# Audio tower on one core: first norm's statistics ahead of the second state scan, transposed rows evicted ahead of the output's exponentials, last tile's sums three chunks earlier

## The chip, the cores and the metric

One core of a Trainium2 chip runs the whole kernel as one program on TensorE (PE), VectorE (DVE), ScalarE (ACT), GpSimd (POOL) and SyncE (SP), which only issues DMAs. The metric is device microseconds (us); the median over several executions is compared. The profile is one more execution, taken with the hardware profiler.

## The reference, cut to what matters

The input is 32 sequences of 750 frames with 256 channels. Two wavelet levels (8 taps, stride 2) give 192 tokens a sequence, 6144 in all. Then come a layer norm, a gated linear recurrence over time, and a second layer norm with a mixture of 8 experts of which each token takes 2.

```
h = tok(x)                                   # two strided convolutions over time
h = h + attn(layernorm(h))
h = h + ffn(layernorm(h))

# attn: k = x Wk, v = r = x Wr, then for each channel over time t
#   y_t = (a + e^(u + k_t) v_t) / (b + e^(u + k_t))     (a, b: running weighted sums, kept stable by a running max)
#   a, b = e^w a + e^k_t v_t,  e^w b + e^k_t ;  out = sigmoid(r) * y ;  out Wo
# ffn: logits = x router_w + router_b; the best 2 of 8 experts, softmax over their 2 logits
#   sum over the 2 of gate * (relu(x W1_e + b1_e) W2_e + b2_e)
```

## The kernel before

The program has two parts, `tokens_to_experts` (up to 333 us in the trace) and `experts` (the rest).

**The first part** goes over 16 pairs of sequences, 384 tokens each, in a software pipeline with five steps. In round i, `body(p0, p1, p2, p3, p4)` works on pair i as p0 (convolutions, first norm, transposes), on pair i-1 as p1 (products with Wk and Wr, running maximum, decays, sum of the weights), on pair i-2 as p2 (the second state scan `weighted_sum`, numerator, `output`, product with Wo, second norm's statistics), on i-3 as p3 (second norm applied, router logits, the choice of two experts) and on i-4 as p4 (ranks by small matmuls, places in the experts' lists, which POOL scatters by indirect DMA). After round 15 four rounds of `drain` empty the pipeline; they are called drain rounds 16 to 19 here. Each engine has its own `body` and `drain`: what is written there is its order, and semaphores join the engines. Nothing is scheduled by a planner.

The names to follow, with the lines at which the trace shows them: on DVE `statistic_1` and `mean_1` (L839, L843: mean and variance of the first norm, for three blocks of 128 tokens), `shift_1` (L858; it also is the line of `shift_2`), `weighted` (L909), `new_ends` (L1000), `weighted_sum` (L913, a scan), `numerator` (L918), `output` (L924), `running_max` (L870, a scan), `difference` (L876), `weights_sum` (L884, a scan), `divisor` (L890), `log_sum` (L903), `statistic_2` and `mean_2` (L849, L853), the choice from `lg_in` (L929) to `selected` (L991), and `places` (L996). On ACT `hidden_in` (L459, evicts the convolution), `root_1` (L477, L479; it waits for all three `mean_1`), `decays` (L529, L532; waits for `difference`), `now` (L537), `log_sigmoid` (L541), `xnT_in` (L506, evicts the transposed rows), `log_divisor` (L545) and `norm_2` (L499). On PE `conv` (L667), `kr` (L694, four products a pair: the first needs `xnT_in`), `ranks` (L703 to L707, between the first and the second `kr`, needs `selected`), `transpose_1` and `transpose_2` (L649), `logits` (L736), `carry` and `project` (L685, L675).

**The second part** goes over 31 tiles of 512 or 256 tokens of one expert. For each of 8 chunks c of 128 hidden units PE makes `up` (L1548) and, two chunks behind, `down` (L1560); ACT evicts with a ReLU (L1511), and DVE splits the result into a high and a low part (L1834, L1836). The sums of the tile before are taken out of PSUM by DVE's `sums` (L1640) at chunk 2 of a 512-row tile and at chunk 5 of a 256-row tile, scaled by ACT's `gated` (L1498) at chunk 3 or 6, and added to the result in DRAM by POOL's `send` (L1465), one indirect DMA for 128 rows. The last tile has 256 rows (2 blocks), the one before it 512 (4 blocks); `send_last` (L1473) sends the last tile's two blocks, and first waits until the four of the tile before have landed.

## Time and profile before

| | us |
|---|---|
| median of 3 runs | 996.16 (995.74 to 1002.78) |
| profiled execution, its own time | 999.81 |
| its span, first to last instruction | 997.9 |
| mean granted TensorE clock, share of full | 0.971 |

| engine | busy us | share of the span |
|---|---|---|
| PE | 915.5 | 92% |
| DVE | 781.4 | 78% |
| ACT | 617.0 | 62% |
| POOL | 567.1 | 57% |

The shares are averages over both parts. In the second part PE is busy nearly without a pause; in the first part no engine is, and each round is a chain through several of them. A start time below is in us from the span's start. Consecutive instructions of an engine overlap a little in the trace, so the step from start to start is shorter than a duration.

### The profile page before, as it was taken

Reading aid. Unit: us, or ns where it says so; the run is one execution under the profiler, and the core shown is the slowest. Engines: PE = TensorE matmul, PEld = TensorE weight load, DVE = VectorE, ACT = ScalarE, POOL = GpSimd, SP = SyncE. Lnnn points to the kernel's source line nnn. Section 1 sums busy time; section 2 is a strip of 40 time slices with the busy share of each in tenths; the row PEclk is TensorE's granted clock in tenths of the full one; section 3 lists DMA queues with packets and bytes.
Section 4 is the critical chain, followed back from the end, with each engine's and each line's share of the span. In section 5 each row is a group of like instructions: output and inputs, shape, how many; then the busy total and the mean of one; then the engine's idle time right before and its main releaser. Section 6 shows DMA issues by size and latency. Waiting matters only on the chain. (4 is left out here: it accounts for less than half of the span.)

```text
span 997.9 us, 17255 instructions
## 1 busy us (share of the span) xinstructions
PE 915.5 (92%) x5838; PEld 782.3 (78%) x5838; DVE 781.4 (78%) x2020; ACT 617.0 (62%) x1182; POOL 567.1 (57%) x463
## 2 busy tenths in 40 slices
PE   4899989898885799999999999999999999999993
PEld 3465656566554699989989998999998999999893
DVE  2589999999998687777877778797787787878762
ACT  2699898998986255455655545565565564556541
POOL 1114465577765646665756764775665675677533
PEclk9999999999987799999999999999999999999998
DMA  9624445367223245554646655556555655565622
GB/s 302 233 80 132 143 131 161 99 208 201 79 61 121 66 171 162 143 133 127 147 129 175 191 132 139 144 147 213 138 142 155 191 150 140 130 198 128 173 36 32
DMA packets 73296, 144.32 MB, mean 145 GB/s; under 512 B 9069, under 2 KB 62430, under 8 KB 69242
## 3 DMA queue, kind: packets, MB, share of 16 engines
q0 software_dynamic: 31136, 99.92, 37.1%
q1 hardware_dynamic: 42074, 43.30, 13.8%
q8 instruction: 48, 0.79, 0.3%
q14 instruction: 38, 0.31, 0.1%
HBM read 111.36 MB, written 31.83 MB: 143 GB/s over the span
## 5 line engine op out<-in xcount | busy, mean ns | idle before, releaser
L1511 ACT ACTIVATE hid<-hp,b 128x512 f32<-128x512 f32 (+1 forms) x248 | 158.4, 639 | 251.8 <-PE hp L1548 225.4
L1560 PE MATMUL acc<-whi,hhi 128*128 128x256 f32 x876 | 245.7, 280 | 0.0
L1560 PE MATMUL acc<-wlo,hhi 128*128 128x256 f32 x876 | 245.4, 280 | 0.0
L1560 PE MATMUL acc<-whi,hlo 128*128 128x256 f32 x876 | 245.3, 280 | 0.0
L1465 POOL DMA_INDIRECT out_rows<-yout,dest x108 | 184.1, 1705 | 48.8 <-issue 48.8
L1548 PE MATMUL hp<-xhi,whi 128*128 128x512 f32 (+1 forms) x496 | 186.2, 376 | 5.6 <-ACT hid L1511 3.1
L1834 DVE CAST hhi<-hid 128x512 fp32r<-128x512 f32 (+1 forms) x240 | 102.7, 428 | 112.0 <-ACT hid L1511 101.0
L1548 PE MATMUL hp<-xlo,whi 128*128 128x512 f32 (+1 forms) x496 | 183.7, 370 | 0.0
L1548 PE MATMUL hp<-xhi,wlo 128*128 128x512 f32 (+1 forms) x496 | 183.2, 369 | 0.0
L1560 PEld LDWEIGHTS acc<-wlo,hhi 128*128 128x128 f32 x876 | 165.3, 189 | 8.4
L1560 PEld LDWEIGHTS acc<-whi,hhi 128*128 128x128 f32 x876 | 164.6, 188 | 8.0
L168 POOL DMA_INDIRECT expert_lists<-tokens,slots x96 | 124.7, 1299 | 72.8 <-DVE slots L1096 43.1
L1594 DVE TENSOR_TENSOR wlo<-h,whi 128x512 fp32r<-128x512 f32 x240 | 162.9, 685 | 3.0 <-ACT whi L1491 3.0
L1560 PEld LDWEIGHTS acc<-whi,hlo 128*128 128x128 f32 x876 | 165.0, 188 | 0.0
L1491 ACT ACTIVATE whi<-h 128x512 fp32r<-128x512 f32 x240 | 147.9, 624 | 27.5 <-DMA h<-in_ew,idx 27.5
L1836 DVE TENSOR_TENSOR hlo<-hid,hhi 128x512 fp32r<-128x512 f32 (+1 forms) x240 | 152.1, 634 | 8.2
L183 POOL DMA_INDIRECT h<-token_rows,tile_tid x110 | 121.0, 1100 | 61.3 <-issue 60.8
L1548 PEld LDWEIGHTS hp<-xlo,whi 128*128 128x128 f32 x496 | 93.8, 189 | 16.3
L1548 PEld LDWEIGHTS hp<-xhi,whi 128*128 128x128 f32 x496 | 93.9, 189 | 15.4 <-ACT hid L1511 3.9
L1548 PEld LDWEIGHTS hp<-xhi,wlo 128*128 128x128 f32 x496 | 93.9, 189 | 8.8
L177 POOL DMA_INDIRECT tile_tid<-expert_lists,idx x31 | 32.0, 1033 | 119.6 <-DVE idx L188 104.7
L694 PE MATMUL kr_ps<-xnT,wk 128*128 128x384 f32 x128 | 54.7, 558 | 27.6 <-ACT xnT L506 27.6
(219 smaller groups left out, 1453.9 us busy)
## 6 DMA issues: line engine op xcount, KB each, us to landing
frames<-in_x SPq DMA_DIRECT2D x32, 512.0 KB
frames<-in_x SPq DMA_DIRECT2D x32, 256.0 KB
token_rows<-xs SPq DMA_DIRECT2D x16, 388.5 KB
out_rows<-h SPq DMA_DIRECT2D x16, 384.0 KB
expert_lists<-setup SPq DMA_DIRECT2D x12, 280.0 KB
h<-token_rows,tile_tid POOLq DMA_INDIRECT x110
out_rows<-yout,dest POOLq DMA_INDIRECT x110
expert_lists<-tokens,slots POOLq DMA_INDIRECT x96
```

What stands on the lines that cost most here:

```text
L168: self.pool.indirect_dma_start(self.lists, bass.IndirectOffsetOnAxis(t.slots[:, q.q, c:c + 1], 0), t.tokens[:, q.q, c % 3, :], None).then_ ...
L177: self.pool.indirect_dma_start(t.tid[:, j.s, 0:j.r, :].rearrange("p r a -> p (r a)"), None, self.groups[j.r], bass.IndirectOffsetOnAxis(t. ...
L183: self.pool.indirect_dma_start(t.xg[:, j.s, r, :], None, self.rows_of[0:upto, :], bass.IndirectOffsetOnAxis(t.tid[:, j.s, r, 0:1], 0)).the ...
L694: last = pe.matmul(kr_ps[m][:, 0:PAIR_TOK], (wk, wr)[j // 2][:, k, m * P:(m + 1) * P], xnT[:, k, :], start=k == 0, stop=k == HC - 1)
L1465: pool.indirect_dma_start(out[:, :], bass.IndirectOffsetOnAxis(dest[:, j.i, r:r + 1], 0), yout[:, j.s, r, :], None, compute_op=ALU.add).th ...
L1491: act.activation(whi[j.s][:, a], raw[:, j.s, a], ACT.Copy).then_inc(whi_done, 1)
L1511: act.activation(hid[:, c % 2, 0:j.r * P], hp[c % 2][:, 0:j.r * P], ACT.Relu, bias=b1[:, j.s, c:c + 1]).then_inc(hid_done, 1)
L1548: last = pe.matmul(hp[c % 2][:, 0:j.r * P], w_[j.s][:, at:at + P], x_[j.s][:, k, 0:j.r * P], start=n == 0, stop=n == 3 * HC - 1)
L1560: last = pe.matmul(acc_of(j, r), h_[:, c % 4, r * P:(r + 1) * P], w_[j.s][:, at:at + C], start=c == 0 and n == 0 and (r % 2 == 0 or j.last ...
L1594: dve.tensor_tensor(wlo[j.s][:, a], raw[:, j.s, a], whi[j.s][:, a].bitcast(F32), ALU.subtract).then_inc(wlo_done, 1)
L1834: dve.tensor_copy(hhi[:, c % 4, 0:j.r * P], hid[:, c % 2, 0:j.r * P]).then_inc(hhi_done, 1)
L1836: dve.tensor_tensor(hlo[:, c % 4, 0:j.r * P], hid[:, c % 2, 0:j.r * P], hhi[:, c % 4, 0:j.r * P].bitcast(F32), ALU.subtract).then_inc(hlo_ ...
```

## The change

Six edits; no instruction is added or taken away.

1. ACT, rounds 0 to 15: `xnT_in(p0)` comes right after `decays(p1)`, ahead of `now` and `log_sigmoid`.
2. DVE, rounds 0 to 15: the three `statistic_1` and the three `mean_1` come ahead of `weighted` and `weighted_sum`; `shift_1` comes ahead of `output`.
3. DVE, drain rounds 16 to 18: the choice of p3 is woven between `statistic_2`, `mean_2` and the steps of p1 or, in round 17, the low parts of the first tile's weights. `selected` ends the round: it comes behind `log_sum` in round 16 and behind `statistic_2` and `mean_2` in round 17.
4. DVE and ACT, last tile: `sums` of the tile before at chunk 2 instead of 5, `gated` at chunk 3 instead of 6.
5. POOL, last tile but one: `send` waits for each block of 128 rows ahead of its DMA, not for all four ahead of the first.
6. POOL, last tile: its wait for `y_taken`, which guarded a gather that the last tile doesn't have, is gone.

```diff
@@ ACT body
                 if p1:
                     sigmoid_exp(p1)
                     decays(p1)
+                xnT_in(p0)
+                if p1:
                     now(p1)
                     log_sigmoid(p1)
-                xnT_in(p0)
@@ DVE body
                 if p3:
                     shift_2(p3)
-                statistic_1(p0, 0)
-                if p2:
-                    weighted(p2)
+                for t in range(3):
+                    statistic_1(p0, t)
                 if p4:
                     new_ends(p4)
+                for t in range(3):
+                    mean_1(p0, t)
+                if p2:
+                    weighted(p2)
...
                 if p2:
                     weighted_sum(p2)
...
-                statistic_1(p0, 1)
...
-                statistic_1(p0, 2)
-                mean_1(p0, 0)
...
-                if p2:
-                    numerator(p2)
+                shift_1(p0)
...
-                mean_1(p0, 1)
-                mean_1(p0, 2)
                 if p2:
                     output(p2)
...
-                shift_1(p0)
                 if p1:
                     running_max(p1)
@@ POOL
-                if p.exists():
-                    pool.wait_ge(y_taken, j.rows())
-                    end_of_waits()
                 if n.exists():
+                    if p.exists():
+                        pool.wait_ge(y_taken, j.rows())
+                        end_of_waits()
                     gather_b2(n)
...
             def send(j):
-                pool.wait_ge(y_ready, j.rows(j.r))
+                if not j.nxt().last():
+                    pool.wait_ge(y_ready, j.rows(j.r))
...
                 for r in range(j.r):
+                    if j.nxt().last():
+                        pool.wait_ge(y_ready, j.rows(r + 1))
@@ ACT, second part
-                    if c == (6 if j.small() else 3) and p.exists():
+                    if c == (6 if j.small() and not j.last() else 3) and p.exists():
                         gated(p)
@@ DVE, second part
+            def sums_at(j):
+                return 5 if j.small() and not j.last() else 2
...
-                    if c == (5 if j.small() else 2) and p.exists():
+                    if c == sums_at(j) and p.exists():
                         sums(p)
```

DVE's queue in a full round, before: from `shift_2` over the second state scan (`sa`) to the running maximum (`pp`). `st` and `mv` are the first norm's statistics and means, `oT` is the output.

```order
L858 SCALAR_TENSOR_TENSOR nb<-mv,rs 128x3
L839 BN_STATS st<-h 128x6
L909 TENSOR_TENSOR e2sv<-es,v 128x772
L1000 TENSOR_TENSOR region_ends<-cnt_ps,region_ends 128x8
L913 SCALAR_TENSOR_TENSOR sa<-es,e2sv 128x772
L839 BN_STATS st<-h 128x6 x2
L843 BN_AGGR mv<-st 128x2
L918 TENSOR_TENSOR num<-t,sa 128x768
L843 BN_AGGR mv<-st 128x2 x2
L924 TENSOR_TENSOR oT<-num,inv 128x768
L858 SCALAR_TENSOR_TENSOR nb<-mv,rs 128x3
L870 SCALAR_TENSOR_TENSOR pp<-wseq,kpad 128x772
```

The same stretch of DVE's queue after the change (the line numbers are one higher there).

```order
L859 SCALAR_TENSOR_TENSOR nb<-mv,rs 128x3
L840 BN_STATS st<-h 128x6 x3
L1001 TENSOR_TENSOR region_ends<-cnt_ps,region_ends 128x8
L844 BN_AGGR mv<-st 128x2 x3
L910 TENSOR_TENSOR e2sv<-es,v 128x772
L914 SCALAR_TENSOR_TENSOR sa<-es,e2sv 128x772
L919 TENSOR_TENSOR num<-t,sa 128x768
L859 SCALAR_TENSOR_TENSOR nb<-mv,rs 128x3
L925 TENSOR_TENSOR oT<-num,inv 128x768
L871 SCALAR_TENSOR_TENSOR pp<-wseq,kpad 128x772
```

The small steps that stood between `e2sv`, `sa` and `num` have gone ahead of them; the three now follow each other directly, each reading what the one before wrote.

The end of DVE's drain round 16 and the start of round 17, before: `sel` is the last step of the choice, `sbb` and `den` belong to p1, `place` reads the ranks that PE makes from `sel`.

```order
L991 TENSOR_TENSOR sel<-oh 128x24
L849 BN_STATS st<-wo_ps 128x6 x3
L853 BN_AGGR mv<-st 128x2 x3
L884 SCALAR_TENSOR_TENSOR sbb<-es 128x772
L890 SCALAR_TENSOR_TENSOR den<-ey,sbb 128x768
L898 SCALAR_TENSOR_TENSOR t<-ey,v 128x768
L903 TENSOR_TENSOR den<-den,er 128x768
L996 TENSOR_TENSOR place<-cnt_ps,region_ends 128x24
```

The same end of DVE's round 16 after the change.

```order
L885 SCALAR_TENSOR_TENSOR sbb<-es 128x772
L973 TENSOR_SCALAR xs<-i 128x3
L977 SCALAR_TENSOR_TENSOR cand<-eq,eid 128x24
L891 SCALAR_TENSOR_TENSOR den<-ey,sbb 128x768
L982 TENSOR_REDUCE i<-cand 128x3
L899 SCALAR_TENSOR_TENSOR t<-ey,v 128x768
L988 TENSOR_TENSOR oh<-cand,i 128x24
L904 TENSOR_TENSOR den<-den,er 128x768
L992 TENSOR_TENSOR sel<-oh 128x24
L997 TENSOR_TENSOR place<-cnt_ps,region_ends 128x24
```

`sel` now stands directly ahead of `place`, with nothing between them on DVE.

DVE's queue in the last tile, after the change: its third chunk, the four sums of the tile before, the fourth chunk. Before, the four stood behind the sixth chunk.

```order
L1875 CAST hhi<-hid 128x256
L1877 TENSOR_TENSOR hlo<-hid,hhi 128x256
L1678 TENSOR_TENSOR ysum<-acc,b2s 128x256 x4
L1875 CAST hhi<-hid 128x256
L1877 TENSOR_TENSOR hlo<-hid,hhi 128x256
```

They moved ahead by three chunks, six instructions of DVE.

## Rows read from the trace of the kernel before

**Rows 1.** Waits over the whole span: total us, times, longest us.

```profile
ACT lv L477 <- DVE mv L843: 18.0, 15, 2.9
ACT dist L529 <- DVE dl L876: 5.5, 15, 1.6
DVE place L996 <- PE cnt_ps L707: 1.5, 2, 0.7
```

**Rows 2.** Timeline of ACT, round 11: start, duration, operation, idle before and releaser.

```profile
209.03 1.12 ACT L529 ACTIVATE dist<-dl,nw 128x384 f32<-128x384 f32 x2 [0.20 <-DVE dl L876]
...
212.59 1.10 ACT L537 ACTIVATE ey<-dl,u 128x384 f32<-128x384 f32 x2
...
214.34 0.84 ACT L506 ACTIVATE xnT<-kr_ps 128x384 f32<-128x384 f32 x2
...
216.93 0.79 ACT L459 ACTIVATE h<-conv_ps 128x768 f32<-128x768 f32 x1
```

**Rows 3.** Timeline of DVE in the same round.

```profile
200.50 0.43 DVE L839 BATCH_NORM_STATS2 st<-h 128x6 f32<-128x256 f32 x1
200.84 0.95 DVE L909 TENSOR_TENSOR e2sv<-es,v 128x772 f32<-128x772 f32 x1
201.70 0.16 DVE L1000 TENSOR_TENSOR region_ends<-cnt_ps,region_ends 128x8 f32<-128x8 f32 x1
201.82 1.77 DVE L913 TENSOR_TENSOR_SCAN sa<-es,e2sv 128x772 f32<-128x772 f32 x1
203.51 0.73 DVE L839 BATCH_NORM_STATS2 st<-h 128x6 f32<-128x256 f32 x2
...
204.23 0.92 DVE L918 TENSOR_TENSOR num<-t,sa 128x768 f32<-128x768 f32 x1
205.07 0.24 DVE L843 BATCH_NORM_AGGREGATE mv<-st 128x2 f32<-128x6 f32 x2
205.23 0.92 DVE L924 TENSOR_TENSOR oT<-num,inv 128x768 f32<-128x768 f32 x1
...
206.15 1.76 DVE L870 TENSOR_TENSOR_SCAN pp<-wseq,kpad 128x772 f32<-128x772 f32 x1
...
208.04 0.96 DVE L876 TENSOR_TENSOR dl<-kpad,pp 128x768 f32<-128x768 f32 x1
...
212.72 1.77 DVE L884 TENSOR_TENSOR_SCAN sbb<-es 128x772 f32<-128x772 f32 x1 [0.65 <-issue]
```

**Rows 4.** Timelines: PE's first product in round 12, DVE's scan in 12, PE in 13.

```profile
215.23 1.56 PE L694 MATMUL kr_ps<-xnT,wk 128*128 128x384 f32 x4 [1.55 <-ACT xnT L506]
...
224.84 1.77 DVE L870 TENSOR_TENSOR_SCAN pp<-wseq,kpad 128x772 f32<-128x772 f32 x1 [1.35 <-issue]
...
233.93 2.93 PE L694 MATMUL kr_ps<-xnT,wk 128*128 128x384 f32 x4 [2.99 <-ACT xnT L506]
```

**Rows 5.** Timeline of DVE in drain rounds 17 to 19.

```profile
320.75 1.10 DVE L849 BATCH_NORM_STATS2 st<-wo_ps 128x6 f32<-128x256 f32 x3 [1.69 <-PE wo_ps L675]
...
323.14 0.16 DVE L858 SCALAR_TENSOR_TENSOR nb<-mv,rs 128x3 f32<-128x3 f32 x1 [0.80 <-ACT rs L479]
...
331.93 0.18 DVE L991 TENSOR_TENSOR sel<-oh 128x24 bf16<-128x24 f32 x1
332.59 0.18 DVE L996 TENSOR_TENSOR place<-cnt_ps,region_ends 128x24 f32<-128x24 f32 x1 [0.48 <-issue]
```

**Rows 6.** Timelines of ACT, DVE and POOL in the last tile, in this order.

```profile
973.86 0.47 ACT L1511 ACTIVATE hid<-hp,b 128x256 f32<-128x256 f32 x1 [0.96 <-PE hp L1548]
...
978.54 1.70 ACT L1498 ACTIVATE yout<-ysum,gate 128x256 f32<-128x256 f32 x4
...
983.09 1.04 ACT L1498 ACTIVATE yout<-ysum,gate 128x256 f32<-128x256 f32 x2 [2.50 <-DVE ysum L1869]
...
977.91 1.41 DVE L1640 TENSOR_TENSOR ysum<-acc,b2s 128x256 f32<-128x256 f32 x4
...
981.84 1.55 POOL L1465 DMA_INDIRECT out_rows<-yout,dest  x1 [15.92 <-issue]
...
992.01 1.55 POOL L1473 DMA_INDIRECT out_rows<-yout,dest  x1 [3.05 <-DMA out_rows<-yout,dest]
```

More of the change, by code:

```diff
@@ L1102, in body @@
                     shift_2(p3)
-                statistic_1(p0, 0)
+                for t in range(3):
+                    statistic_1(p0, t)
+                if p4:
+                    new_ends(p4)
+                for t in range(3):
+                    mean_1(p0, t)
                 if p2:
                     weighted(p2)
-                if p4:
-                    new_ends(p4)
+                if p4 and p4.q == KNOWN - 1:
+                    whole_tiles()
                 if p2:
@@ L1121, in body @@
                 if p4 and p4.q == KNOWN - 1:
+                    not_reached()
+                shift_1(p0)
+                if p4 and p4.q == KNOWN - 1:
                     first_places_of_tiles()
                     first_experts()
-                mean_1(p0, 1)
-                mean_1(p0, 2)
                 if p2:
@@ L1228, in drain @@
                     running_max(p1)
+                    lg_in(p3)
                     difference(p1)
+                    best(p3)
                     sigmoid_divisor(p1)
-                if p2 and not p1:
+                    is_best(p3)
+                    best_numbers(p3)
+                    statistic_2(p2, 0)
+                    first_number(p3)
+                    statistic_2(p2, 1)
+                    is_first(p3)
+                    statistic_2(p2, 2)
+                    other_logits(p3)
+                    mean_2(p2, 0)
+                    second(p3)
+                    mean_2(p2, 1)
+                    is_second_best(p3)
+                    mean_2(p2, 2)
+                    margin(p3)
+                    weights_sum(p1)
+                    first_expert(p3)
+                    second_numbers(p3)
+                    divisor(p1)
+                    second_number(p3)
+                    value_now(p1)
+                    is_second(p3)
+                    log_sum(p1)
+                    selected(p3)
+                elif p2:
                     taken()
@@ L1256, in drain @@
                     selected(p3)
-                if p2 and not p1:
-                    first_weights(range(3, 6))
-                if p2:
-                    for t in range(3):
-                        statistic_2(p2, t)
-                    for t in range(3):
-                        mean_2(p2, t)
-                if p1:
-                    weights_sum(p1)
-                    divisor(p1)
-                    value_now(p1)
-                    log_sum(p1)
             rounds(body, drain)
```

31 lines of the change are left out of this document (25 added, 6 removed).

## The prediction

> **What bounds the kernel now.** I read four views: the waits over the whole span, to see which engine stands for whom; the timelines of ACT and DVE through one full round of the first part; the timelines of the drain rounds; and the chain that ended last with the timelines of the last tile. Three edits lie in the first part and three in the last two tiles; the tiles in between, where PE works without a pause, keep their order.
>
> The waits show what the change aims at: ACT stands 15 times, 18.0 us in all, for the first norm's means [rows 1]. But right behind it stands a second wait, also 15 times: ACT's `decays` waits for DVE's `difference`, 5.5 us in all. The round is a ring of two engines. `decays` starts as the difference ends (208.04 + 0.96 = 209.00, start 209.03) [rows 2, 3]. ACT then works through to the next `hidden_in`, which starts at 216.93 and ends at 217.72: 8.69 us. DVE's `statistic_1` starts 0.04 later, and from there to the end of the difference DVE has no pause: 200.50 to 209.00, 8.50 us [rows 3]. The sum, 8.69 + 0.04 + 8.50 + 0.03 = 17.26 us, is the round. ACT's wait for the means lies between `hidden_in` and `decays`, where ACT is ahead of DVE in any case; taken away, it comes back as a longer wait ahead of `decays`. What counts is DVE's stretch from the first statistic to the difference.
>
> **The change, part by part.**
>
> *DVE in a full round.* The instructions are the same; what changes is what stands between dependent ones. An instruction that needs nothing of the one before starts 0.08 us before that one ends (scan 201.82 + 1.77 = 203.59, next at 203.51); one that reads its result starts 0.03 after (200.84 + 0.95 = 201.79, scan at 201.82) [rows 3]. So a dependent pair costs 0.11 us unless a small step fills it. Before, from the first statistic to the running maximum: 206.15 - 200.50 = 5.65. After, in order: three statistics 0.34 + 0.32 + 0.32 = 0.98 (0.64 for the pair from its start to `mean_1`'s), `new_ends` 0.09, three means at 0.08 = 0.24, `weighted` 0.98 to the dependent scan, the scan 1.77 + 0.03, `numerator` 0.92 + 0.03 with `shift_1` inside it, `output` 0.85: 5.88. That is 0.23 more a round; without `new_ends` (rounds 2 and 3) 0.14. In round 10 the early tables' steps fill the gaps, and I count nothing.
>
> Rounds 2 to 10: 2 x 0.14 + 6 x 0.23 = 1.7 us. In round 12 the scan stands 1.35 us for POOL's seeds, behind a scatter that itself hangs on round 10 [rows 4]; that swallows what rounds 11 and 12 add (0.46). Rounds 13 to 15: 3 x 0.23 = 0.7.
>
> A rule of the Trainium skill speaks for another size here: "VectorE: DVE Perf Modes", section "The DRAIN you can't avoid", says that a semaphore between consecutive Vector instructions costs nothing extra, because each waits for the pipeline to empty anyway. By it the order of dependent steps is free, the 2.4 us above would be 0, and the time 990.3. The trace doesn't agree: 0.03 us after the end against 0.08 before it [rows 3]. It is the second rival below.
>
> *ACT's earlier `xnT_in`.* The eviction starts at 212.59 instead of 214.34, 1.75 us earlier. It is 0.84 long, 0.74 less the overlap, and delays `now`, whose end goes from 213.69 to 214.43; `divisor` needs it, but stands behind the scan `weights_sum`, which ends at 214.49 [rows 2, 3]. So it costs nothing, by 0.1 us. What it gives: PE's first `kr` starts sooner, but the next thing in PE's queue is `ranks`, which needs `selected` at the end of DVE's round. In most rounds nothing further moves. Twice `places` waits for the ranks, 1.5 us in all [rows 1]: in round 13, where PE had stood 2.99 us for `xnT` and then took 2.93 us for a product that takes 1.56 elsewhere, the lower of its two clock levels by the pace [rows 4], and in drain round 16. Both waits go: -1.5 us.
>
> *Drain rounds.* In round 16 `selected` moves behind `log_sum`, directly ahead of `places`, which needs PE's ranks of it. From `selected` to `places` is 332.59 - 331.93 = 0.66 us [rows 5], where `places` could follow `log_sum` at once: +0.65. It delays `shift_2`, `norm_2`, the logits and `project` behind them. The gaps that the weaving fills in round 16 lie beside ACT's chain from `decays` to `log_divisor`, for which `log_sum` waits: 0. In round 17 DVE stands 1.69 us for `project` ahead of `statistic_2` [rows 5]; before, the whole choice was done by then. Now `selected` is about 2.05 us behind the first `statistic_2` (three statistics of 0.34, the rest small steps of 0.05 to 0.21, estimated from the steps of rows 3 and the dependent pair); with 0.66 to `places`, 0.2 to `new_ends` and 0.1 it lets `shift_2` start 3.0 us behind the statistic. Before it started 323.14 - 320.75 = 2.39 behind: +0.6. Queued behind it is the last `norm_2`, and all of rounds 18 and 19.
>
> Sum of the first part: 1.7 - 1.5 + 0.7 + 0.65 + 0.6 = +2.1 us. Cover that may be gone: where PE's clock stays low. The same product takes 1.56 at one pace and 2.93 at the other [rows 4]; in the drains some ten such groups lie on the chain, so a shifted low stretch is worth up to 3 us either way.
>
> *The last tile.* `gated` follows the fourth eviction instead of the seventh: it starts at 973.86 + 0.38 = 974.24 instead of 978.54, if the sums are there. They start at about 977.91 less three chunks, (978.54 - 0.38 - 973.86) = 4.30, so 973.61, and the first is there by 974.0. That is -4.30. POOL then waits for the first block, 0.43 us after the start, not for all four, 1.70 after it: -1.27 [rows 6]. From POOL's first DMA to the end nothing changes: four issues, the landing, for which the second group stands 3.05 us, two issues, the landing, 981.84 to 997.9. The last tile's own blocks are scaled by 983.09 + 1.04 = 984.13, and its second group would now be issued at 992.01 - 5.57 = 986.4, so they don't bind. PE keeps its pace: DVE's fourth chunk comes 0.6 us later, ACT's fifth 0.6, and `down` runs two chunks behind. Together -5.6 us. Bounds: POOL's pick-up, 981.84 - 980.24 = 1.60 before, might be half of that or cost a little for each of three more waits: +-0.8.
>
> Net: +2.1 - 5.6 = -3.5 us. Against the profiled execution's own 999.81 that is 996.3; it lay 3.65 above the median, so on the median, 996.16, it is **992.7 us**.
>
> **The rivals.**
>
> 1. *ACT's wait is on the ring.* Then all 18.0 us go with it: 996.2 - 18.0 - 5.6 = 972.6, faster by 2.4%. For it: the wait is the largest of ACT's in this part. Against it: `decays` waits for DVE in each of the same 15 rounds. 7%.
> 2. *The order of dependent steps is free* (the rule above). No cost in the full rounds, otherwise as forecast: 990.3. 12%.
> 3. *The tail doesn't move.* POOL's gap of 15.92 ends for another reason than `y_ready`; then the first part's cost remains, 998.3. Against: the DMA comes 1.60 after the last of four scalings. 6%.
> 4. *PE's clock falls in every round* (the other side). PE's pause of 1.55 us, today ahead of the first product [rows 4], then lies ahead of `ranks`. If that brings the low clock seen after 2.99 us of standing, three products behind it take 1.37 more each, 4.1 us, against 1.5 us that PE has to spare: 2.6 x 14 = 36 us, 1029. It decides once PE loses more than those 1.5 us a round. Against: pauses of the same total have left the clock at full in the plain rounds. 4%.
>
> **How the numbers follow.** The forecast has 71%. Its own range is 988.5 to 996.5: 3 us of clock, 0.8 of pick-up, 1 of the dependent pairs. The whole range takes in rivals 2 and 3: 987.5 to 998.5. About 1%, 10 us, is what a measurement of this kernel tells from no change. Faster by more (below 986.2): rival 1 and a little of low clock gone, 8%. Slower by more (above 1006.1): rival 4, 4%. Within 1%: 88%.
>
> **What would show it.** In the profile of the changed kernel: the wait of ACT's `root_1` for the means near 0, and `decays`' wait for the difference at 1.3 us a round or more; the step from one `hidden_in` to the next 17.5 instead of 17.26; PE's `ranks` standing for `selected`; `places` in round 13 without a wait, in drain round 17 with one; `shift_2` of round 18 about 3.0 behind the statistic; the second part as long as before; the first of the last tile's `yout` at about 4 us ahead of where it was, counted from the tile's first chunk, and 16 us from POOL's first DMA to the end. A shorter step between the `hidden_in` would make the prediction wrong on the fast side, low clock in the full rounds on the slow side.

## The result, and the profile after

| | before | after |
|---|---|---|
| median, us | 998.13 (15 runs) | 994.65 (15 runs) |
| lowest to highest, us | 995.11 to 1002.78 | 992.35 to 996.17 |
| span of the profiled execution, us | 997.9 | 993.8 |
| mean granted TensorE clock | 0.971 | 0.970 |

The ratio is 0.9969, with a 95% interval of 0.9956 to 0.9982: 3.1 us faster, 1.8 to 4.4. The forecast was 3.5 us faster, and "within 1%". The time that it named, 992.7 us, was counted from 996.16, the median of the first three runs of the kernel before; over fifteen runs that median is 998.13, so 994.65 lies 2 us above the forecast time, inside its range of 988.5 to 996.5. The two spans differ by 4.1 us, but not where the forecast put them. I cut both traces at the first `hidden_in`, the last one (round 15), the first matmul of the second part, ACT's eviction of the last tile's fourth chunk, and the end.

| stretch, us | before | after | difference | forecast |
|---|---|---|---|---|
| first to last `hidden_in` | 253.59 | 256.17 | +2.6 | +1.6 |
| to the second part's first matmul (drain) | 63.78 | 66.03 | +2.3 | +0.5 |
| to the last tile's fourth chunk | 639.09 | 636.98 | -2.1 | 0 |
| to the end | 24.04 | 17.20 | -6.8 | -5.6 |

The differences add up to -4.1. The forecast's +2.1 for the first part is divided here by its terms: 1.7 and 0.7 for the full rounds, less the wait of `places` that lies in them (half of 1.5); then 0.65 and 0.6 for the drain, less the other half. So a forecast that was nearly right in the sum put the first part's cost too low and the tail's gain too small, and in the profile 2 us of the second part, whose instructions the change left alone, came on top. The experiments below take these apart.

The waits over the whole span of the kernel after (us in all, times, longest) answer to [rows 1]:

```profile
ACT dist L529 <- DVE dl L877: 20.0, 15, 2.0
ACT lv L477 <- DVE mv L844: 1.6, 1, 1.6
```

ACT's wait for the means is gone but for the first round (18.0 before), and the wait ahead of `decays` has grown from 5.5 to 20.0 us. The wait has moved, as forecast; it wasn't removed.

DVE's timeline through a plain full round of the kernel after (start, duration, operation), answering to [rows 3]:

```profile
167.75 1.08 DVE L840 BATCH_NORM_STATS2 st<-h 128x6 f32<-128x256 f32 x3
168.74 0.15 DVE L1001 TENSOR_TENSOR region_ends<-cnt_ps,region_ends 128x8 f32<-128x8 f32 x1
168.81 0.30 DVE L844 BATCH_NORM_AGGREGATE mv<-st 128x2 f32<-128x6 f32 x3
169.03 0.93 DVE L910 TENSOR_TENSOR e2sv<-es,v 128x772 f32<-128x772 f32 x1
169.99 1.79 DVE L914 TENSOR_TENSOR_SCAN sa<-es,e2sv 128x772 f32<-128x772 f32 x1
171.82 0.96 DVE L919 TENSOR_TENSOR num<-t,sa 128x768 f32<-128x768 f32 x1
172.69 0.15 DVE L859 SCALAR_TENSOR_TENSOR nb<-mv,rs 128x3 f32<-128x3 f32 x1
172.81 0.97 DVE L925 TENSOR_TENSOR oT<-num,inv 128x768 f32<-128x768 f32 x1
173.70 1.75 DVE L871 TENSOR_TENSOR_SCAN pp<-wseq,kpad 128x772 f32<-128x772 f32 x1
...
175.59 0.96 DVE L877 TENSOR_TENSOR dl<-kpad,pp 128x768 f32<-128x768 f32 x1
```

From the first statistic to the running maximum it is 173.70 - 167.75 = 5.95 us, where it was 5.65 and the forecast said 5.88; to the end of the difference 8.80 instead of 8.50. The step from one `hidden_in` to the next is 17.56 instead of 17.26, the same 0.30. ACT's stretch, from `decays` to the end of the next `hidden_in`, is 8.69 us in both.

ACT's timeline shows that two rounds were longer still:

```profile
113.70 0.79 ACT L459 ACTIVATE h<-conv_ps 128x768 f32<-128x768 f32 x1
...
131.80 0.79 ACT L459 ACTIVATE h<-conv_ps 128x768 f32<-128x768 f32 x1
```

18.10 from the one to the other, where the next is 17.56; the round from 202.80 to 220.90 is the other one of 18.10. In both, PE's clock is at its lower level for a while, and the granted clock of a window that takes in such a stretch lies below 1.00. These are PE's timeline in the one, the table of windows (the columns ahead of the last three are PE, PEld, DVE, ACT and POOL busy; then PE's clock, the DMA share and GB/s), and DVE's timeline in the other:

```profile
115.34 2.77 PE L695 MATMUL kr_ps<-xnT,wr 128*128 128x384 f32 x4
...
114.00:117.00 3.00, 3.00 (x7) 1.71 (x7) 2.96 (x12) 3.00 (x8) 2.39 (x3) 0.65 0.98 254
200.00:207.00 7.00, 5.21 (x17) 2.68 (x16) 6.90 (x19) 6.61 (x14) 5.75 (x6) 0.76 0.61 172
...
209.13 0.16 DVE L859 SCALAR_TENSOR_TENSOR nb<-mv,rs 128x3 f32<-128x3 f32 x1 [0.47 <-ACT rs L479]
```

The four products that take 1.46 us elsewhere in this round take 2.77. `x2T_in`, with which ACT evicts the transposed rows of the second norm, is then late, `root_1` behind it too, and `shift_1`, which now stands ahead of `output` and the running maximum on DVE, waits 0.47 us for it. Before, `shift_1` stood behind `output`, with the numerator and `output` to cover a late `root_1`. The change has put a new wait into the ring, one that shows only where PE is slow. What it costs beyond what the old order pays in such a round is seen in e8.

DVE's timeline in the drain, in rounds 16 and 17, answering to [rows 5]:

```profile
299.55 0.18 DVE L930 TENSOR_TENSOR lg<-cnt_ps,rbs 128x24 f32<-128x24 f32 x1 [0.80 <-PE cnt_ps L737]
...
310.07 0.17 DVE L992 TENSOR_TENSOR sel<-oh 128x24 bf16<-128x24 f32 x1
310.73 0.18 DVE L997 TENSOR_TENSOR place<-cnt_ps,region_ends 128x24 f32<-128x24 f32 x1 [0.48 <-PE cnt_ps L708]
...
324.47 0.43 DVE L850 BATCH_NORM_STATS2 st<-wo_ps 128x6 f32<-128x256 f32 x1 [2.79 <-PE wo_ps L676]
...
327.16 0.18 DVE L997 TENSOR_TENSOR place<-cnt_ps,region_ends 128x24 f32<-128x24 f32 x1 [0.48 <-PE cnt_ps L708]
327.46 0.16 DVE L859 SCALAR_TENSOR_TENSOR nb<-mv,rs 128x3 f32<-128x3 f32 x1
```

`places` comes 0.66 us behind `selected`, and in round 18 `shift_2` comes 327.46 - 324.47 = 2.99 us behind the first statistic: both as forecast. The first row is not in the forecast. `lg_in` now stands ahead of `difference`, and it waits 0.80 us for the logits (PE's clock was low from 289.0 to 295.8) and holds `difference` up.

The last tile, ACT and then POOL, answering to [rows 6]:

```profile
976.60 0.47 ACT L1549 ACTIVATE hid<-hp,b 128x256 f32<-128x256 f32 x1 [0.96 <-PE hp L1586]
976.97 1.70 ACT L1536 ACTIVATE yout<-ysum,gate 128x256 f32<-128x256 f32 x4
...
977.93 1.55 POOL L1503 DMA_INDIRECT out_rows<-yout,dest  x1 [9.28 <-ACT yout L1536]
```

The scaling starts 0.37 us behind the fourth chunk instead of 4.68, which is 4.31, the forecast's 4.30. POOL's first DMA starts 0.96 behind the start of the scaling instead of 3.30, a gain of 2.34 where the forecast had 1.27. From that DMA to the end it is 15.9 us (16.1 before).

### The profile page after: what moved, and what is told of

It reads as the page before. It is cut to its first block and busy times, and to the rows that moved or that the text cites. A ratio compares the mean times of both kernels' runs of the same rounds, so it can differ in the third digit from the quotient of the medians.

```text
span 993.8 us, 17254 instructions
## 1 busy us (share of the span) xinstructions
PE 917.6 (92%) x5838; PEld 782.6 (79%) x5838; DVE 783.1 (79%) x2020; ACT 616.4 (62%) x1182; POOL 544.9 (55%) x463
## 5 line engine op out<-in xcount | busy, mean ns | idle before, releaser
L168 POOL DMA_INDIRECT expert_lists<-tokens,slots x96 | 116.6, 1214 | 99.6 <-DVE slots L1097 70.6
L1536 ACT ACTIVATE yout<-ysum,gate 128x256 f32<-128x256 f32 x110 | 47.4, 499 | 19.8 <-DVE ysum L1678 17.3
## 6 DMA issues: line engine op xcount, KB each, us to landing
frames<-in_x SPq DMA_DIRECT2D x32, 256.0 KB, 6.4
```

The source lines that it names most:

```text
L168: self.pool.indirect_dma_start(self.lists, bass.IndirectOffsetOnAxis(t.slots[:, q.q, c:c + 1], 0), t.tokens[:, q.q, c % 3, :], None).then_ ...
L1536: act.activation(yout[:, j.s, r, :], ysum[:, j.s, r, :], ACT.Copy, scale=gate[:, j.i, r:r + 1]).then_inc(y_ready, 1)
```

## The experiments

Each kernel is an edit of one of the two. The runs stand in three groups of four; each group had its own runs of the kernel before, with medians of 997.62, 1005.73 and 997.98 us, so a kernel is compared by its ratio, and across groups only by that. The second group is e5 to e8. Why the kernel before took 8 us longer there isn't known, as it wasn't profiled there, so what is compared across groups stands less firmly than what is compared within one. Each kernel has 10 to 14 runs, but e12 has 6 and e11 only 2. The theory that they test: the full round is a ring, ACT from `decays` to `hidden_in` and DVE from the first statistic to the difference; the body edits lengthen DVE's half, the drain edit puts `selected` on the path, and the tail gains more than both lose. The rival accounts: ACT's waits were on the ring, the order of dependent steps is free, and the tail doesn't move.

The table gathers what the twelve showed: the ratio with its interval, the difference that it makes of 998 us, and from each profile the step of a plain round and the four stretches of the section above.

| kernel | ratio (95%) | us | step | rounds | drain | second part | end |
|---|---|---|---|---|---|---|---|
| before | 1 | | 17.26 | 253.6 | 63.8 | 639.1 | 24.0 |
| after | 0.9969 (0.9956 to 0.9982) | -3.1 | 17.56 | 256.2 | 66.0 | 637.0 | 17.2 |
| e1 tail | 0.993 (0.9907 to 0.9954) | -7.0 | 17.26 | 253.6 | 64.6 | 639.5 | 17.6 |
| e2 full rounds | 1.0022 (1.0002 to 1.0043) | +2.2 | 17.57 | 256.0 | 62.9 | 637.9 | 24.2 |
| e3 drain | 0.9996 (0.9975 to 1.0018) | -0.4 | 17.26 | 253.6 | 65.5 | 635.4 | 24.1 |
| e4 DVE's order | 1.0025 (1.0004 to 1.0047) | +2.5 | 17.56 | 256.5 | 63.4 | 638.0 | 24.3 |
| e5 early rows, tail | 0.9909 (0.9875 to 0.9943) | -9.1 | 17.26 | 253.1 | 62.5 | 640.7 | 17.3 |
| e6 with small steps between | 0.9952 (0.9924 to 0.9979) | -4.8 | 17.36 | 256.1 | 62.7 | 638.1 | 17.3 |
| e7 no drain edit | 0.9944 (0.9908 to 0.998) | -5.6 | 17.56 | 257.4 | 63.9 | 639.8 | 17.5 |
| e8 two steps moved | 0.9923 (0.9896 to 0.995) | -7.7 | 17.26 | 252.8 | 63.3 | 640.7 | 17.4 |
| e9 early sums | 0.995 (0.9932 to 0.9969) | -5.0 | 17.26 | 251.6 | 63.3 | 638.0 | 19.9 |
| e10 block waits | 0.9973 (0.9954 to 0.9992) | -2.7 | 17.26 | 251.9 | 63.3 | 637.6 | 21.6 |
| e11 short `weighted` | 0.9836 (0.9795 to 0.9876) | -16.4 | 16.73 | 247.0 | 61.9 | 637.4 | 17.5 |
| e12 both halves shorter | 0.9894 (0.9868 to 0.9921) | -10.6 | 17.17 | 251.2 | 63.2 | 639.6 | 17.4 |

### e1: the tail alone

The diff's hunks on POOL and on the second part (edits 4 to 6), and nothing else.

> The kernel before with only edits 4 to 6 (last tile's sums and scaling at the early chunk, the send block by block, the dropped wait). My theory, from the whole change's profile: from the last tile's fourth chunk to the end 24.04 us become 17.2, so the kernel is 6.8 us faster than the kernel before (5.6 by the prediction, 6.8 by what the profile of the change shows). Rival, the tail doesn't move and the whole gain of the change came from elsewhere (a later transfer of weights that PE no longer waited for): 0 us. The first part's steps between the hidden_in stay at 17.26.

Measured: 7.0 us faster (4.6 to 9.3). The end is 17.6 us instead of 24.0. The rival falls: the tail moves, and by more than the whole change.

### e2: the full rounds alone

Edits 1 and 2, without the drain's and the tail's.

> The kernel before with only the full rounds' edits 1 and 2 (ACT's early transposed rows, DVE's statistics ahead of the scan). My theory: the step between two hidden_in is 17.5 to 17.6 instead of 17.26, the POOL wait of round 12 and the places waits swallow some of it, and the last hidden_in is 2.3 to 2.6 us later; the kernel is 1 to 3 us slower than before. Rival, ACT's 18.0 us of waits for the means were on the ring: 18 us faster. Rival, the order of dependent steps is free: no difference, or 1.5 us faster by the dropped waits of places.

Measured: 2.2 us slower (0.2 to 4.3), a step of 17.57, 256.0 us of rounds. Two rivals fall here. Had ACT's 18.0 us been on the ring, this kernel would be 18 us faster. Had the order of dependent steps been free, the step would be 17.26. The two rounds of 18.1 are there as well, at the same places as in the kernel after.

### e3: the drain alone

Edit 3.

> The kernel before with only edit 3, the choice of experts woven into the drain rounds. My theory: selected directly ahead of places costs 0.65 us in round 16 and 0.6 in round 17, so the second part's first matmul is 1.2 us later; with it a wait of DVE's difference behind the logits in round 16 if PE's clock is low there (up to 0.8 more). 1 to 2 us slower. Rival, weaving fills gaps between dependent small steps and gives them back: 0 to 1 us faster.

Measured: the time can't be told from before (2.5 us faster to 1.8 slower). The profile says more. DVE's timeline, rounds 16 and 17:

```profile
294.58 0.18 DVE L929 TENSOR_TENSOR lg<-cnt_ps,rbs 128x24 f32<-128x24 f32 x1 [0.36 <-PE cnt_ps L736]
...
305.11 0.17 DVE L991 TENSOR_TENSOR sel<-oh 128x24 bf16<-128x24 f32 x1
305.76 0.18 DVE L996 TENSOR_TENSOR place<-cnt_ps,region_ends 128x24 f32<-128x24 f32 x1 [0.48 <-PE cnt_ps L707]
...
319.13 0.43 DVE L849 BATCH_NORM_STATS2 st<-wo_ps 128x6 f32<-128x256 f32 x1 [2.42 <-PE wo_ps L675]
...
322.11 0.16 DVE L858 SCALAR_TENSOR_TENSOR nb<-mv,rs 128x3 f32<-128x3 f32 x1
```

The edit alone brings all three costs: 0.65 from `selected` to `places`, 2.98 instead of 2.39 to `shift_2`, and a wait for the logits ahead of `difference`. The drain is 65.5 us, where the four profiles with the old drain and the old rounds (before, e1, e9, e10) have 63.3 to 64.6, mean 63.7: +1.8. The rival, that weaving gives something back, has no sign in the drain's rows, but the time doesn't exclude it.

### e4: DVE's order without the early rows

Edit 2 alone.

> The kernel before with only edit 2 (DVE's order in the full rounds; ACT's transposed rows stay behind log_sigmoid). My theory: the round's step is 17.5 as with both edits, because PE's first product is not on the ring; the waits of places in round 13 and drain round 16 stay (1.5 us), so it is 1 to 2 us slower than with both edits, 3 to 4 slower than before. Rival: the early transposed rows cost what they give, and it ends equal to the kernel with both.

Measured: 2.5 us slower (0.4 to 4.7); beside e2's 2.2 that is no difference that the times can tell. The step is 17.56, so the early `xnT_in` plays no part in it. DVE's row in drain round 16 shows the wait that edit 1 removes:

```profile
293.21 0.18 DVE L996 TENSOR_TENSOR place<-cnt_ps,region_ends 128x24 f32<-128x24 f32 x1 [0.74 <-PE cnt_ps L707]
```

Rounds and drain together are 319.9 us against e2's 318.8, which is 1.0 us of the 1.5 expected for edit 1; e7 below shows that two profiles of one first part can differ by more than that. My 1 to 2 us slower than with both edits is not seen in the times.

### e5: the early rows and the tail

Edit 1 and edits 4 to 6; DVE keeps its old order in the first part.

> The kernel before with edit 1 (ACT's transposed rows ahead of now and log_sigmoid) and the last tile's edits 4 to 6; DVE's order in the full and drain rounds is that of before. My theory: the step between the hidden_in stays 17.26, the waits of places in round 13 and in drain round 16 (0.7 to 0.8 each) go, so it is 0.7 to 1.5 us faster than the tail alone, about 8 us faster than before, and it is the fastest of the versions so far. Rival: edit 1 only moves the low stretches of PE's clock into full rounds, and some round costs 0.5 to 1 us more, so that it ends equal to the tail alone or slower.

Measured: 9.1 us faster (5.7 to 12.5). The step is 17.26, and `places` in drain round 16 stands without a wait:

```profile
285.84 0.18 DVE L997 TENSOR_TENSOR place<-cnt_ps,region_ends 128x24 f32<-128x24 f32 x1
```

The first part, from the first `hidden_in`, takes 315.6 us; the four profiles with the old code have 314.9 to 318.2. Of the rival there is a trace. In the kernel before, e1 and e3 a low stretch at the start of round 13 makes `places` wait, and that round is 0.5 to 0.8 us longer. e5 has no low stretch there, but one in round 11, which is 17.78 us long, 0.52 more than a plain round, and in round 12 `places` stands 0.99 us. So edit 1 costs nothing in a plain round; that it is worth 0.7 to 1.5 us agrees with the time but isn't proven by it.

### e6: statistics ahead, with small steps between

DVE's order in the full round, over e5 (the conditions and the steps of round 10 are left out):

```diff
-statistic_1(p0, 0)
+for t in range(3):
+    statistic_1(p0, t)
 weighted(p2)
 new_ends(p4)
 weighted_sum(p2)
-statistic_1(p0, 1)
-statistic_1(p0, 2)
 mean_1(p0, 0)
 numerator(p2)
 mean_1(p0, 1)
 mean_1(p0, 2)
 output(p2)
 shift_1(p0)
 running_max(p1)
```

> As the run with edit 1 and the tail, and the three statistics ahead of the second state scan too, but with small independent steps left between its dependent ones: weighted, new_ends, scan, mean_1, numerator, two mean_1, output, shift_1. It tells whether the round grew because the statistics went ahead or because the dependent steps of DVE followed each other without a step between. My theory (dependent pairs): the step between the hidden_in is 17.26, not 17.56, and the total that of the run beside it. Rival (the statistics ahead of the scan cost by themselves, since they are now all behind hidden_in and ahead of the scan): 17.5 and 3 us slower than the run beside it.

Measured: a step of 17.34 to 17.37, neither 17.26 nor 17.5, and 4.8 us faster than before, less than e5 (their intervals overlap). 0.10 us a round makes little more than 1 us of the 4.3 between the two; the rest isn't explained, and e6's profiled execution took 991.0 us where its median is 1000.18. DVE's timeline:

```profile
146.40 1.08 DVE L840 BATCH_NORM_STATS2 st<-h 128x6 f32<-128x256 f32 x3
...
148.41 1.77 DVE L914 TENSOR_TENSOR_SCAN sa<-es,e2sv 128x772 f32<-128x772 f32 x1
150.09 0.16 DVE L844 BATCH_NORM_AGGREGATE mv<-st 128x2 f32<-128x6 f32 x1
150.21 0.96 DVE L919 TENSOR_TENSOR num<-t,sa 128x768 f32<-128x768 f32 x1
```

The scan starts 148.41 - 146.40 = 2.01 us behind the first statistic. In [rows 3] it is 1.32, and 1.96 with the 0.64 of the two statistics that now stand ahead of it, so 0.05 of the cost lies there. The other 0.07 is at `numerator`. One small step of 0.16 us lies in the gap, and the pair stays as far apart as with none: it starts 0.03 behind the scan's end and lasts 0.96, where in [rows 3], two statistics and a mean behind the scan, it lasts 0.92. So a small step in a dependent pair is free but doesn't shorten it; only a step longer than the gap of some 0.1 us does. This is the term that the forecast mis-sized: it priced a pair at 0.11 us, and it is 0.11 and, for `numerator` and `output`, about 0.04 of longer duration.

### e7: the change without its drain edit

The kernel after with the drain rounds of before.

> The changed kernel without edit 3: the drain rounds in the order of before, all else changed. My theory: shift_2 of drain round 18 is again 2.4 us behind the statistic, places of round 16 has no wait, the lg_in wait of 0.8 goes, and the second part's first matmul comes 1.2 to 2.5 us earlier than in the changed kernel, counted from hidden_in of round 0 (322.2 there); the time is 1 to 2.5 us lower than the changed kernel's, about 993. Rival: the weaving gave as much as it cost, and the two are equal.

Measured: ratio 0.9944 against the 0.9969 of the kernel after, their intervals overlapping. First `hidden_in` to the second part is 321.3 us against 322.2. The drain is 63.9 instead of 66.0, but its rounds are 257.4 instead of 256.2. Two of them are longer than in the kernel after: round 12 by 0.93, in which `places` stands 0.92 us with the clock full (PE's rows have its ranks done at 220.36, and it starts at 221.74; why stays open), and round 14 by 0.53, in which the clock is low and `shift_1` waits 0.47 us. e2 has the very same first part and took 318.8. By the granted clock of windows of 3 us (each window's share below full, times two, times 3 us) PE was at its lower level for 44 us in e2's profile and for 55 us in e7's, counted to the end of the low stretch in which the second part begins. So two profiles of the very same first part can lie 2.5 us apart, and the drain edit's cost has to be read from the drain: 1.8 us with the old rounds (e3), and 66.0 less the 63.4 of e2 and e7, 2.6 us, with the new ones.

### e8: two small steps out of the stretch

Over e5:

```diff
-second_places(p4)
-lg_in(p3)
 difference(p1)
+second_places(p4)
+lg_in(p3)
```

> As the run with edit 1 and the tail, with second_places and lg_in moved behind difference in the full rounds, that is out of DVE's stretch from the first statistic to the difference into the gap ahead of weights_sum. It tests that this stretch is on the ring: before, difference starts 0.13 us behind the end of running_max with the two steps between them, and would start 0.03 behind without. My theory: the step between the hidden_in is 17.16 instead of 17.26 and it is 1.0 to 1.4 us faster than the run beside it. Rival (the ring is ACT's own queue, which never stands longer than 1.3 us): 17.26 and equal.

Measured: a step of 17.26 and a time like e5's. My theory's number was wrong, but not for the rival's reason. DVE's timeline:

```profile
155.37 1.76 DVE L871 TENSOR_TENSOR_SCAN pp<-wseq,kpad 128x772 f32<-128x772 f32 x1
157.26 0.96 DVE L877 TENSOR_TENSOR dl<-kpad,pp 128x768 f32<-128x768 f32 x1
158.14 0.17 DVE L1071 TENSOR_TENSOR pl<-place,oh 128x24 f32<-128x24 f32 x1
```

With nothing between them the difference starts 1.89 us behind the start of the running maximum, the same as in [rows 3] with two small steps between. It starts 0.13 behind the scan's end either way. The stretch didn't get shorter, so the run says nothing on the ring; e11 was made for that.

It says something on the new wait. Its round 11 has a low stretch at the same place as the kernel after: 1.0 us behind `hidden_in`, with a granted clock of 0.60 from 202 to 205 us, where the kernel after has 0.9 us and 0.61 from 203 to 206. `x2T_in` stands 1.17 us for PE in either. ACT's and DVE's timelines in e8:

```profile
206.59 0.49 ACT L512 ACTIVATE x2T<-tp_ps 128x384 f32<-128x384 f32 x1 [1.17 <-PE tp_ps L650]
...
213.38 0.43 DVE L850 BATCH_NORM_STATS2 st<-wo_ps 128x6 f32<-128x256 f32 x1 [0.97 <-PE wo_ps L676]
```

In the old order `shift_1` has no wait here, but `statistic_2` then stands 0.97 us for `project` (0.42 in the kernel after), and the round is 17.75 long, 0.49 more than a plain one. In the new order it is 18.10, 0.54 more. So in this round the new wait takes the place of another, and costs 0.05 us.

### e9 and e10: the tail in halves

e9 is edit 4 alone, e10 edits 5 and 6 alone.

> The kernel before with edit 4 alone: last tile's sums and scaling at the early chunk; POOL still waits for all four blocks. It splits the 6.8 us that the tail gained. My theory: the scaling starts 4.3 us earlier relative to the last tile's fourth chunk, and POOL's first DMA stays 3.3 us behind the start of the scaling, so 4.3 to 4.5 us faster. Rival: the blocks must be sent one by one for the early sums to show, since the four issues and the landing of the last but one tile end the kernel: 0 to 2.

> The kernel before with edits 5 and 6 alone: POOL waits for each block ahead of its DMA, the sums stay at the late chunk. My theory: POOL's first DMA comes 0.96 us behind the start of the scaling instead of 3.30, as in the changed kernel, so 2.3 us faster. The prediction's figure for this edit was 1.27; rival: that figure, with 1.60 us from the first block's end to the DMA.

Measured: 5.0 us faster (3.1 to 6.8) and 2.7 us faster (0.8 to 4.6); the end is 19.9 and 21.6 us instead of 24.0, so 4.1 and 2.4, which add up to e1's 6.5. ACT and POOL in e9, then in e10:

```profile
970.23 1.70 ACT L1498 ACTIVATE yout<-ysum,gate 128x256 f32<-128x256 f32 x4
973.53 1.55 POOL L1465 DMA_INDIRECT out_rows<-yout,dest  x1 [11.63 <-issue]
...
975.17 1.70 ACT L1501 ACTIVATE yout<-ysum,gate 128x256 f32<-128x256 f32 x4
976.13 1.55 POOL L1468 DMA_INDIRECT out_rows<-yout,dest  x1 [13.58 <-ACT yout L1501]
```

In e9 the DMA starts 1.60 us behind the end of the last scaling, as before the change. In e10 it starts 976.13 - (975.17 + 0.43) = 0.53 behind the end of the first. e9's rival falls by its time. e10's rival of 1.27 lies inside the interval of e10's time and falls by the profile alone. Where the other 1.07 us went: in the old form POOL takes the wait, then counts up a semaphore of its own (`end_of_waits`), then issues; in the new form that step comes first and the wait stands directly ahead of the DMA. In the trace of before the count stands at 980.3, right behind the last scaling, and the DMA 1.6 us behind it. But the count alone isn't shown to be the 1.07 us: `send_last` has one too, at 991.2, and its DMA starts at 992.01, 0.8 behind. No run moved it by itself, so the cause stays open. Nor does e10 part edit 5 from edit 6. Before, the wait for `y_taken` ended with the last of the four sums, at 977.91 + 1.41 = 979.32, which is later than the first scaling's end, 978.54 + 0.43 = 978.97, so with edit 5 alone that wait could have held the first block back.

### e11: the ring made shorter

Over e5, from the second pair on `weighted` works on 96 of its 772 columns:

```diff
-dve.tensor_tensor(flat(e2sv), flat(e2s), flat(v), ALU.mult)
+n = 772 if q.q < 1 else 96
+dve.tensor_tensor(flat(e2sv)[:, 0:n], flat(e2s)[:, 0:n], flat(v)[:, 0:n], ALU.mult)
```

It leaves out most of the product, so it serves for the timing alone.

> As the run with edit 1 and the tail, but weighted multiplies only 96 of its 772 columns from the second pair on (the rest of its result is left out), so that DVE's stretch from the first statistic to the difference gets about 0.8 us shorter and nothing changes on ACT, which has 1.28 us of waits in the same stretch. It tests the ring in the direction that the moved small steps did not reach. My theory (ACT from decays to hidden_in, then DVE from the first statistic to the difference): the step between the hidden_in is 16.45 instead of 17.26. Rival (ACT's own queue or PE's sets the round, with DVE only by chance as long): 17.1 to 17.26.

Measured: a step of 16.73 in the plain rounds (16.56 in rounds 3 and 4), and, from two runs, 16.4 us faster than before (12.4 to 20.5), of which 9.1 are e5's. DVE's timeline, and one row of POOL's:

```profile
144.32 0.43 DVE L840 BATCH_NORM_STATS2 st<-h 128x6 f32<-128x256 f32 x1
144.67 0.24 DVE L911 TENSOR_TENSOR e2sv<-es,v 128x96 f32<-128x96 f32 x1
...
149.20 0.16 DVE L859 SCALAR_TENSOR_TENSOR nb<-mv,rs 128x3 f32<-128x3 f32 x1
149.43 1.77 DVE L871 TENSOR_TENSOR_SCAN pp<-wseq,kpad 128x772 f32<-128x772 f32 x1
...
151.33 0.96 DVE L877 TENSOR_TENSOR dl<-kpad,pp 128x768 f32<-128x768 f32 x1
...
149.13 0.21 POOL L393 TENSOR_TENSOR kpad<-kpad,c_before 128x4 f32<-128x4 f32 x1
```

The multiplication got 0.71 us shorter, not the expected 0.8, and the running maximum now starts 0.23 behind the start of `shift_1` (0.07 before). The 0.16 between is a wait for POOL's seed, which ends at 149.34. In rounds 3 and 4, where that wait is absent, the stretch is 0.71 and the step 0.70 shorter. From the first statistic to the difference's end it is 7.97 instead of 8.50, and the step is 16.73 instead of 17.26: both 0.53. With +0.30 (the kernel after), +0.10 (e6) and -0.53 the step has followed DVE's stretch in both directions by its full amount, with ACT's half at 8.69 or 8.70 us in all of them. The ring is shown; the rival that the round is ACT's own or PE's falls.

### e12: both halves shorter by order alone

Over e5, on ACT and on DVE:

```diff
 # ACT body
 hidden_in(p0)
+root_2(p3)
...
 log_divisor(p1)
-root_2(p2)
 # DVE body
 places(p4)
+statistic_1(p0, 0)
 shift_2(p3)
-statistic_1(p0, 0)
...
 second_numbers(p3)
+mean_2(p2, 2)
+second_number(p3)
+is_second(p3)
+selected(p3)
 weights_sum(p1)
-second_number(p3)
 divisor(p1)
-is_second(p3)
-mean_2(p2, 2)
 value_now(p1)
-selected(p3)
 log_sum(p1)
```

In the drain ACT's `root_2(p3)` opens a round instead of `root_2(p2)` closing the one before, which is the same order.

> As the run with edit 1 and the tail, and both halves of the ring shortened by order alone: root_2 (0.43 us of ACT) goes from ahead of hidden_in to behind it, with shift_2 behind the first statistic_1; and DVE's small steps mean_2, second_number, is_second and selected go from between weights_sum and log_sum into the 0.65 us that DVE stands ahead of weights_sum. My theory: about 0.3 us a round of DVE's work leaves the stretch from weights_sum to the first statistic, ACT's falls by 0.4, and the step is 16.9 to 17.0 instead of 17.26: 3 to 4 us faster than the run with edit 1 and the tail, if PE's clock does as before. Rival: only ACT's half or only DVE's half shortens (each hides the other's gain): 17.2 and equal.

(`root_2` is ACT's step between `mean_2` and `shift_2`, for the second norm what `root_1` is for the first.)

Measured: 10.6 us faster than before (7.9 to 13.2), the fastest of the kernels that do all the work, though its interval overlaps e5's and e8's. The step is 17.17, a third of the expected gain and nearer to the rival's 17.2. DVE's timeline:

```profile
158.88 0.18 DVE L992 TENSOR_TENSOR sel<-oh 128x24 bf16<-128x24 f32 x1
159.07 1.77 DVE L885 TENSOR_TENSOR_SCAN sbb<-es 128x772 f32<-128x772 f32 x1
...
163.00 0.96 DVE L904 TENSOR_TENSOR den<-den,er 128x768 f32<-128x768 f32 x1 [0.20 <-ACT den L545]
```

The small steps do fill the gap: the scan `weights_sum` starts behind them without a wait. But `log_sum` now waits 0.20 us for ACT's `log_divisor`, which stands behind four other ACT operations. DVE's half is tied to ACT a second time, inside the round, and this second tie now binds: the first statistic starts 0.30 us behind the end of `hidden_in`, where it was 0.03, though ACT's half has fallen from 8.69 to 8.28. e12 against the kernel after is 0.9894 against 0.9969, and the intervals don't touch: it beats both kernels, the kernel after by a comparison across groups.

## Why the prediction came out right

**What bounds the round** held. Taking away ACT's 18.0 us of waits brought none of it (e2: 2.2 us slower), and the wait came back ahead of `decays`, 1.38 us in a plain round where I had written 1.3. The ring stands on three lengths of DVE's stretch, with e11 as its test from the other side.

**The dependent pairs** held in sign, but not in size: 0.30 us a round instead of 0.23. The rule that I weighed against the trace, the Trainium skill's "VectorE: DVE Perf Modes", section "The DRAIN you can't avoid", would have made the step 17.26 in the kernels after, e2, e4 and e7. It was 17.56 or 17.57 in all four; the trace doesn't agree with it. My own price of a pair was short by the 0.04 us by which a dependent instruction also lasts longer, and I took a small step for a cure of the pair, where e6 shows that it is merely free inside it.

**The rounds that the sum left out** are the larger miss of the first part. The forecast saw no risk in `shift_1` ahead of `output`. With a low stretch of PE's clock in rounds 6 and 11 the round is 0.54 us longer, in each of the kernels after, e2 and e7 (and in round 14 of e7). I had noted that a shifted low stretch is worth up to 3 us, but for the drains only. The new wait is read from the trace, but it isn't the only way in which a low stretch costs: in e5 and e6, where `shift_1` stands behind `output`, a round with one was 0.52 and 0.37 us longer too (in e5 DVE's `statistic_2` stood 1.29 us for `project`), while the low stretch at 60 us in the kernel before cost nothing. e8 has the old order and the low stretch at the same place of round 11, and paid 0.49 there, so of that round's 0.54 only 0.05 is the new order's. Round 6 has a low stretch in the three kernels with edits 1 and 2 (after, e2, e7) and in no other; whether the change brings it there stays open, and with it 0.5 of the 1.1 us.

**Round 12** was no firm cover. I let POOL's wait of 1.35 us swallow what rounds 11 and 12 add. In the kernel after it was gone; but in e9 and e10, whose first part is that of before, it was gone too (17.47 us for that round where the profile of before has 18.70). It is there again in e6, e11 and e12. It comes and goes between executions, and with it up to 2 us of any two profiles' difference in the rounds (253.6 in three of those profiles, 251.6 and 251.9 in two).

**`xnT_in`** cost nothing, as forecast, and `places` lost its wait in drain round 16 (e5 against e4). In round 13 the low stretch which caused that wait was itself not always there.

**The drain**: both terms for `selected` came out as computed, 0.66 us for the distance and 2.99 us against the 3.0 for `shift_2`. What was missed was `lg_in` ahead of `difference`, up to 0.80 us. I had looked at the weaving for gaps that it could fill and written zero, and not for what it puts ahead of `difference`. By the profiles the edit costs 1.8 to 2.6 us; e3's time alone doesn't confirm it, so on the device's time this stays open.

**The last tile**: 4.30 was right (4.31 in the trace, 5.0 with its interval of 3.1 to 6.8 in e9's time). The waits by block gave 2.34 instead of 1.27, beyond the 0.8 of my bound, because I took POOL's pick-up of 1.60 us to be the same behind a shorter wait. It became 0.53, for a reason that stays open (e10).

**The second part**, forecast as unchanged, was 2.1 us shorter in the one profile. This is not shown to be an effect of the change: it ranges from 635.4 to 640.7 us over the fourteen profiles, though all run the same instructions in that stretch. Yet the two shortest, 635.4 and 637.0, are those of the two kernels with the drain edit (e3 and after), so a link with edit 3 isn't excluded; it would also account for e3's time, which doesn't show the drain's cost. The length of this part goes with how long PE stands for the ReLU's output, behind which ACT waits for a transfer of weights. The waits from 345 to 965 us, in e3, the kernel after and e5 in this order:

```profile
PE hp L1584 <- ACT hid L1547: 1.1, 3, 0.7
...
PE hp L1586 <- ACT hid L1549: 1.7, 3, 0.6
...
PE hp L1552 <- ACT hid L1515: 3.4, 5, 1.2
PE hp L1552 <- issue: 1.6, 3, 0.7
```

With 1.1, 1.7 and 5.0 us of waiting these parts last 635.4, 637.0 and 640.7.

So the measured -3.1 us came about by a tail that gives 7.0 (forecast 5.6) and a first part that costs more than 2.1 (4.8 in the profile). By their own medians the three parts, -7.0, +2.2 and -0.4, add up to -5.2. The 2 us between that and -3.1 are within the intervals of three such runs, about 2.3 us each. The total was right; the two terms behind it were each too small by 1 to 3 us, with opposite signs. The mechanism was foreseen, but that the total came so close is in part luck.

## What to carry to other kernels

Find the ring of two engines before pricing a wait: a wait on the engine that is ahead costs nothing, and removing it moves it to the next meeting point. Before moving small steps away from between large dependent ones, check what they were hiding; and before putting a step that waits for another engine ahead of the large ones, price it for the round in which that engine is slow, not for the plain one, and against what the old order pays in that same round. Of a change in several parts, time each part alone: here the tail alone gave 7.0 us, and all three parts together 3.1.

## What the runs showed of the hardware beyond this

- Where `numerator` reads the scan's result directly behind it, it starts 0.03 us after the end and lasts 0.96 us instead of 0.92; a small independent step of 0.16 us between them changes neither (e6). With two small steps between, `output` lasts 0.92 ([rows 3]). An independent instruction starts 0.08 us before the end of the one ahead. That it is the dependence which makes the second longer isn't shown: `weighted`, which reads neither neighbour, lasts 0.93 us in the kernel after, 0.95 before and 0.97 in e6 (medians).
- Behind two of the scans (`running_max` with `difference`, `weights_sum` with `divisor`) the dependent step starts 0.13 us after the end, with two, one or no small steps between; behind `weighted_sum` it is 0.03 to 0.04. What makes the difference stays open.
- POOL's DMA comes 0.53 us behind the ACT operation that it waits for in the form with the wait directly ahead of it (after, e1, e10), and 1.60 us in the form with a semaphore step of POOL's own between (before, e9).
- The same program's first part took 318.8 us with 44 us at PE's lower clock (e2), and 321.3 us with 55 (e7); 0.9 of the difference lies in round 12, where the clock was full.
